# A gated delta rule in front of a mixture of experts: token-major rows with the head's parity on the partition halves

## The reference, cut to what matters

```python
q, k, v = (short_conv_silu(x @ W, conv) for W, conv in ...)   # x: layer-normed, 4 taps over tokens
q, k = l2norm(q), l2norm(k)                                   # per head
beta = sigmoid(x @ Wb)                                        # one number per token and head
for each token:                                               # the delta rule, state S is 64x64 per head
    u = beta * (v - k @ S);  S = S + outer(k, u);  o = (q / 8) @ S
o = o * rsqrt(mean(o * o) + 1e-5) * norm_w                    # per head
x = x + o @ Wo
x = x + experts(layernorm(x))                                 # 16 routed experts, top 4, and a shared one
```

## Time and profile before

| what | us |
|---|---|
| three runs | 1413.03, 1421.60, 1421.83; median 1421.6 |
| the profiled execution | 1421.09 |
| its span, first to last instruction | 1419.3 |
| around the span | 1.8 |
| TensorE busy | 1325.8 (93% of the span) |
| DVE busy | 865.7 (61%) |
| ACT busy | 372.2 (26%) |
| first hop, last hop (start of the first product) | 128.5, 604.4 |
| mean granted clock of TensorE | 0.963 of 2.4 GHz |

### The profile page before, as it was taken

The page is one execution under the profiler, slowest core; times in us unless marked ns, Lnnn a source line. Parts: engine busy times, 40 slices in busy tenths (PEclk is TensorE's granted clock), DMA queues, the critical chain, the costliest instruction groups (busy, mean ns, idle before and its releaser), DMA issues.

```text
span 1419.3 us, 27137 instructions
## 1 busy us (share of the span) xinstructions
PE 1325.8 (93%) x8434; PEld 836.9 (59%) x8435; DVE 865.7 (61%) x2394; ACT 372.2 (26%) x794; POOL 349.6 (25%) x422
## 2 busy tenths in 40 slices
PE   5968998999999779998999989999999999999996
PEld 4757776887687546554444445555555555555553
DVE  3797578458754711543511157777777777777774
ACT  3544545354454223312000001111111111111111
POOL 1202313132322212311455202122221222222211
PEclk9988999899898889999999999999999999999998
DMA  4204543754366961126545735666667555565430
GB/s 150 46 15 115 88 111 86 150 104 89 98 131 159 250 140 41 43 85 210 184 179 217 240 70 127 131 130 134 133 154 165 127 126 124 121 145 75 73 53 4
DMA packets 208386, 171.06 MB, mean 121 GB/s; under 512 B 71344, under 2 KB 160432, under 8 KB 208304
## 3 DMA queue, kind: packets, MB, share of 16 engines
q1 hardware_dynamic: 134928, 114.16, 30.1%
q0 software_dynamic: 16496, 34.23, 12.2%
q10 hardware_dynamic: 56880, 21.54, 7.3%
HBM read 91.06 MB, written 82.73 MB: 122 GB/s over the span
## 4 chain that ended last, share of the span: by engine, by line
PE 52%; DVE 1%; issue 1%; POOL 0%; POOLq 0%; ACT 0%; DVEq 0%
PE pD L2007 14%; PE pG L1989 13%; PE pU L1998 13%; PE pD L1977 4%; PE pG L1960 4%; PE pU L1960 3%; DVE ups L1907 1%; PE pU L1954 0%; PE pD L1974 0%; POOLq L1730 0%; DVE xsT L1895 0%; POOL front_region L1784 0%; DVE a L1930 0%; ACT y L1860 0%; ACT ups L1821 0%
## 5 line engine op out<-in xcount | busy, mean ns | idle before, releaser
L1907 DVE STREAM_TRANSPOSE ups<-a 32x96 f32<-32x96 f32 (+1 forms) x1264 | 330.3, 261 | 42.7
L1804 POOL DMA_INDIRECT out<-y,ix x79 | 122.6, 1551 | 491.7 <-ACT y L1860 338.2
L2007 PE MATMUL pD<-w,ups 128*128 (+1 forms) x474 | 219.3, 599 | 3.6 <-DVE ups L1907 3.6
L1989 PE MATMUL pG<-w,xsT 128*128 x632 | 201.5, 461 | 3.0 <-issue 3.0
L1998 PE MATMUL pU<-w,xsT 128*128 x632 | 199.9, 459 | 0.0
L1989 PEld LDWEIGHTS pG<-w,xsT 128*128 128x128 f32 x632 | 120.3, 190 | 92.5 <-issue 42.2
L882 PE MATMUL pProj<-front_region 128*128 128x256 f32 x624 | 162.8, 406 | 2.1 <-ACT front_region L665 1.5
L1998 PEld LDWEIGHTS pU<-w,xsT 128*128 128x128 f32 x632 | 120.1, 190 | 66.9
L2007 PEld LDWEIGHTS pD<-w,ups 128*128 128x128 f32 (+1 forms) x474 | 90.8, 192 | 98.0 <-issue 81.7
L1221 DVE SCALAR_TENSOR_TENSOR front_region<-front_region,cw 128x256 f32<-128x256 f32 x288 | 135.6, 512 | 14.9 <-ACT front_region L679 11.4
L882 PEld LDWEIGHTS pProj<-front_region 128*128 128x128 f32 x624 | 117.9, 198 | 21.9 <-ACT front_region L665 2.1
(11 more groups left out here) (238 smaller groups left out, 1610.5 us busy)
## 6 DMA issues: line engine op xcount, KB each, us to landing
w<-in_up_T SPq DMA_DIRECT2D x16, 1408.0 KB
slot_rows<-zeros SPq DMA_DIRECT2D x79, 266.0 KB
xs<-slot_rows ACTq DMA_DIRECT2D x316, 64.0 KB
w<-in_down_T SPq DMA_DIRECT2D x16, 512.0 KB
front_region<-in_L_attn_hidden_states SPq DMA_DIRECT2D x16, 256.0 KB, 3.6
x2r<-in_L_attn_hidden_states SPq DMA_DIRECT2D x16, 256.0 KB, 4.8
partial_sums<-x2r SPq DMA_DIRECT2D x16, 256.0 KB, 3.2
x_normed<-x2n SPq DMA_DIRECT2D x16, 256.0 KB, 2.2
```

The source lines that it names most:

```text
L1804: pool.indirect_dma_start(out=flat, out_offset=bass.IndirectOffsetOnAxis(ap=ix[1 - par][:, 0:1], axis=0), in_=y[1 - par][:, :], in_offset= ...
L1907: dve.transpose(aT[par][B * to:B * to + B, 0:n, rows], a[rows, 0:len(IC) * P].rearrange("p (c n) -> p c n", c=len(IC))[:, 0:n, B * to:B * ...
L1989: mm = pe.matmul(pG[0][:, 0:I], xsT[par][:, k, :], w[:, bass.ds(slot, 1), 2 * I * k:2 * I * k + I], start=(k == 0), stop=(k == DC - 1))
L2007: mm = pe.matmul(pYq[:, :], aT[1 - par][0:m, c, :], down[0:m, :, UPW + D * c:UPW + D * (c + 1)], start=(c == 0), stop=(c == 2))
```

## The change

Token-major rows get another layout: the partition is now (head's parity f, token within the chunk), and the chunk c lies on the free axis beside n. Everything that holds token-major rows follows: Rs, Us, osb, vh, ktok, NP, TT, PT, and PSUM pC and pG, where the bank is now picked by the chunk c and no longer by f.

- All hops' products read half f and write half f: the two quadrants on the diagonal, f = 0 and 1 in turn, both into bank c. `gram` and `scores` use these two quadrants as well.
- `residual`, `u_copy` and `o_copy` of a chunk are 128x256 and contiguous instead of 64x512 in two banks.
- Each turn of k, q, v and o is 16 products of 64x64 with the identity (an ordinary matmul, two records each, x32) instead of 4 transposes of 128x128 (x4).
- `betas` is 32 products for a pair, each with 64 tokens as the stationary operand and 4 columns moving, where it was 8 with 128 tokens and 8 columns. Wb's columns are permuted on the host.
- The semaphore QS_psum and the wait on it in `hop_o` go; the order of the three groups there stays.

```diff
+    def of_chunk(ap, c):
+        return ap[:, HH * DH * c:HH * DH * (c + 1)]
...
             def u_copy(t, c):
                 act.wait_ge(s_Up, 2 * t + c + 1)
                 least(act, s_Op, 2 * t + c - 1)
-                r = cols(c, C)
-                act.activation(Us[r, :].rearrange("p (f m) -> p f m", f=2), pC[r, :, 0:HH * DH], ACT.Copy).then_inc(s_U, 1)
+                act.activation(of_chunk(Us, c), pC[:, c, 0:HH * DH], ACT.Copy).then_inc(s_U, 1)
...
+            def turn_heads(bank_, src, done):
+                for n in range(HH):
+                    for c in range(2):
+                        for f in range(2):
+                            mm = pe.matmul(bank_[half(f), 0, cols(HH * c + n)], src(n, c, f), ident[half(f), half(f)],
+                                           start=True, stop=True)
+                mm.then_inc(done, 1)
...
                 for h in range(2):
-                    for k in range(DC):
-                        mm = pe.matmul(pT0[:, 0, H * h:H * h + H], xnT[p % 2][:, k, cols(h, P)], wb[:, k, :],
-                                       start=(k == 0), stop=(k == DC - 1))
+                    for c in range(2):
+                        at = H * h + HH * c
+                        for k in range(DC):
+                            for f in range(2):
+                                mm = pe.matmul(pT0[half(f), 0, at:at + HH], xnT[p % 2][:, k, tok(h, c)],
+                                               wb[:, k, HH * f:HH * f + HH], start=(k == 0), stop=(k == DC - 1))
...
-                turn(pT0, lambda m: kq[p % KQ_RING][:, m, tok(t)], s_ktp)
+                turn_heads(pT0, lambda n, c, f: kq[p % KQ_RING][half(f), n, tok(t, c)], s_ktp)
...
                     for c in range(2):
                         for f in range(2):
                             kk = kq[p % KQ_RING][half(f), n, tok(t, c)]
-                            mm = pe.matmul(pG[cols(c, C), f, cols(n)], kk, kk, start=True, stop=True)
+                            mm = pe.matmul(pG[half(f), c, cols(n)], kk, kk, start=True, stop=True)
...
             def hop_u(t, c):
                 pe.wait_ge(s_TT, t + 1)
                 pe.wait_ge(s_R, 2 * t + c + 1)
-                r = cols(c, C)
                 for n in range(HH):
+                    g = HH * c + n
                     for f in range(2):
-                        g = HH * f + n
-                        mm = pe.matmul(pC[r, f, cols(n)], TT[t % TT_RING][r, cols(g)], Rs[r, cols(g)], start=True, stop=True)
+                        mm = pe.matmul(pC[half(f), c, cols(n)], TT[t % TT_RING][half(f), cols(g)], Rs[half(f), cols(g)],
+                                       start=True, stop=True)
...
-                dve.tensor_tensor(half_major(Rs[r, :]), two_banks(pC, r), by_half(vh[t % VH_RING][r, :]), ALU.subtract)\
+                dve.tensor_tensor(of_chunk(Rs, c), pC[:, c, 0:HH * DH], of_chunk(vh[t % VH_RING], c), ALU.subtract)\
```

More of the change, by code:

```diff
@@ L341, in by_head, with by_chunk, two_banks @@
         return ap.rearrange("p (h d) -> p h d", d=DH)
[L343 to L351, removed]
+    def of_chunk(ap, c):
+        return ap[:, HH * DH * c:HH * DH * (c + 1)]
+    def by_chunk(ap):
+        return ap.rearrange("p (c n d) -> p c n d", c=2, d=DH)
+    def two_banks(ps):
+        return ps[:, :, 0:HH * DH].rearrange("p c (n d) -> p c n d", d=DH)
     def heads_of(ap, t, w=DH):
         one = ap[:, H * (t % 2):H * (t % 2) + H]
-        return one.rearrange("p (n f) -> p f n", f=2).unsqueeze(3).to_broadcast([P, 2, HH, w])
+        return one.rearrange("p (c n) -> p c n", c=2).unsqueeze(3).to_broadcast([P, 2, HH, w])
     def quads(ap):
@@ L736, in o_copy @@
                 least(act, s_oTp, t - 1)
-                r = cols(c, C)
-                act.activation(by_half(osb[t % 2][r, :]), two_banks(pC, r), ACT.Copy).then_inc(s_O, 1)
+                act.activation(of_chunk(osb[t % 2], c), pC[:, c, 0:HH * DH], ACT.Copy).then_inc(s_O, 1)
             def o_square(t):
@@ L908, in qT @@
                     pe.wait_ge(s_qsq, t)
-                turn(pT0, lambda m: kq[p % KQ_RING][:, DC + m, tok(t)], s_qtp)
+                turn_heads(pT0, lambda n, c, f: kq[p % KQ_RING][half(f), DC + n, tok(t, c)], s_qtp)
             def vT_turn(t):
@@ L918, in vT_turn @@
                     pe.wait_ge(s_vh, t)
-                turn(pT0, lambda m: vT[:, m, tok(t)], s_vtp)
+                turn_heads(pT0, lambda n, c, f: vT[half(f), n, tok(t, c)], s_vtp)
             def gram(t, u):
@@ L986, in hop_o @@
                 pe.wait_ge(s_U, 2 * t + c + 1)
-                r = cols(c, C)
                 for n in range(HH):
                     for f in range(2):
-                        mm = pe.matmul(pC[r, f, cols(n)], kq[t // 2 % KQ_RING][half(f), DC + n, tok(t, c)],
-                                       S[half(f), cols(n)], start=(n == 0), stop=False, skip_group_check=True)
-                mm.then_inc(s_QS, 1)
+                        pe.matmul(pC[half(f), c, cols(n)], kq[t // 2 % KQ_RING][half(f), DC + n, tok(t, c)],
+                                  S[half(f), cols(n)], start=(n == 0), stop=False, skip_group_check=True)
                 for n in range(HH):
+                    g = HH * c + n
                     for f in range(2):
-                        mm = pe.matmul(pS[half(f), 0, cols(n)], ktok[t % KT_RING][r, cols(2 * n + f)],
-                                       Us[r, cols(HH * f + n)], start=False, stop=False, skip_group_check=True)
+                        mm = pe.matmul(pS[half(f), 0, cols(n)], ktok[t % KT_RING][half(f), cols(g)], Us[half(f), cols(g)],
+                                       start=False, stop=False, skip_group_check=True)
                 mm.then_inc(s_Sp, 1)
-                for f in (c, 1 - c):
-                    if f != c:
-                        pe.wait_ge(s_QS, 2 * t + c + 1)
-                    for n in range(HH):
-                        g = HH * f + n
-                        mm = pe.matmul(pC[r, f, cols(n)], PT[t % 2][r, cols(g)], Us[r, cols(g)], start=False, stop=True,
-                                       skip_group_check=True)
+                for n in range(HH):
+                    g = HH * c + n
+                    for f in range(2):
+                        mm = pe.matmul(pC[half(f), c, cols(n)], PT[t % 2][half(f), cols(g)], Us[half(f), cols(g)],
+                                       start=False, stop=True, skip_group_check=True)
                 mm.then_inc(s_Op, 1)
@@ L1009, in oT_turn @@
                 least(pe, s_x2g, t)
-                turn(pT1, lambda c: osb[t % 2][:, cols(c, P)], s_oTp)
+                for n in range(HH):
+                    for c in range(2):
+                        for f in range(2):
+                            mm = pe.matmul(pT1[half(f), 0, P * n + C * c:P * n + C * c + C],
+                                           osb[t % 2][half(f), cols(HH * c + n)], ident[half(f), half(f)],
+                                           start=True, stop=True)
+                mm.then_inc(s_oTp, 1)
             def out_proj(t):
```

18 lines of the change are left out of this document (9 added, 9 removed).

## The result

| | before | after |
|---|---|---|
| median of 4 runs | 1417.3 | 1437.5 |
| lowest to highest | 1413.0 to 1421.8 | 1431.1 to 1440.7 |
| the profiled execution, its span | 1421.1, 1419.3 | 1431.1, 1429.3 |
| mean granted clock of TensorE | 0.963 | 0.973 |

The ratio is 1.0123, with a 95% interval of 1.009 to 1.0157. By the medians the change costs 15 to 20 us, 0.9 to 1.2%. The forecast was 1430, +8.7: the time lies in its range, on its upper side. The two profiled executions are 10.0 us apart, near the sum; the medians are about twice as far apart as it said.

A forecast was written before the change was run, and what follows sets the result against it. TensorE was taken to set the end in the hops' stretches, DVE during the first inverse. Terms +3 + 15.3 - 6 - 3.6 = +8.7 on the profiled 1421.1 gave 1430 us (own range 1420 to 1440, chance 0.52); overall range 1409 to 1450.

The forecast's parts named there:

- less than twice: Sign that the prediction is wrong: turns on TensorE costing less than twice what they did; 0.93 for 0.44 us was forecast.
- Betas didn't double: Rival: a pair's betas double to 3.7 us and no wait absorbs anything, 1447 us; chance 0.23.
- The halves of one bank don't block each other: Rival it answers: TensorE takes both row halves' products in one bank one after another, 1570 us; chance 0.05.
- the bounds set for them: Signs of being wrong: mean clock from 128 to 630 us moving over 0.02, last inverses' load wait changing over 5 us.
- I take half of those waits, -6: From 110.8 to 440 us, longer TensorE work and shorter Rs fill half of 11.2 us of waits; bounds 0 and -11.
- The third rival: Hops' chain and clock give back more than products cost: shorter waits, a third of clock loss regained, 1414 us; chance 0.20.
- +3 up to 60 us: Opening: four turns of k and two grams, plus shapes, stand ahead of DVE's scaling of the Gram matrices, +3 us.
- nothing from there to 110.8: From 60 to 110.8 us, 7 turns and two grams, some 5 us, lie beside DVE's dense work: nothing.
- the 15.3: Sum from 110.8 to 440 us: turns +20.6, scores and grams +10.1, hops -18.4, shapes +3, before waits.
- From 440 to 505 us nothing was forecast: Turns, grams, scores and hops there sum to +0.6, ahead of a 10.7 us wait set by DVE and transfers: nothing.
- The tail was to give 3.6: From 505 to 630 us: 8 hops -7.4, 5 turns +2.4, 3 scores +1.4, together -3.6 us.
- the 1400 us for the far end of the third: Third rival's far end: half the clock loss regained, tail hops gain 6 us more, 1400; chance beyond 1% faster 0.12.

The follow-up runs named there:

- e8: The changed kernel run again unchanged, 7 runs, as a baseline: 1435.7 us, ratio 1.0092 to before.
- e3: The changed kernel with the old wide betas (128 tokens stationary, 8 columns): 1427.1 us, ratio 1.0057 to before.
- e10: The kernel before with betas alone in the narrow form (64 tokens stationary, 4 columns): 1420.6 us, ratio 0.9982 to before.
- e7: The kernel before with PT Us of a tile's two chunks issued together in turn, one copy osb per tile: 1411.9 us, ratio 0.9935 to before.
- e9: The kernel before with each hop's PT Us issued in turn with the next hop's U: 1426.4 us, ratio 1.0017 to before.
- e11: e9 with the turn of o and its copy oT one slot later: 1418.3 us, ratio 0.9978 to before.
- e12: The kernel e7 run again beside e11: 1409.4 us, ratio 0.9907 to before.
- e6: The changed kernel with each copy Us and osb and each subtraction Rs doubled into an unread scratch tile: 1437.5 us, ratio 1.0105 to before.
- e2: The changed kernel with the turns of k, q and v doing only their first chunk: 1417.2 us, ratio 0.9975 to before.
- e4: The kernel before with each turn of k, q, v and o issued twice: 1439.4 us, ratio 1.0143 to before.
- e5: The changed kernel with every product of gram and scores issued twice: 1456.7 us, ratio 1.0237 to before.
- e1: The changed kernel with products of U and PT Us issued for all even heads, then all odd ones: 1444.5 us, ratio 1.0174 to before.

## Why the prediction came out as it did

**Right, by the rows above.** A quadrant's record costs 0.058 us, and the price of a group is its fullest quadrant: U and PT Us fell by 0.45 to 0.5, gram and scores rose by 0.4 to 0.5, a turn by 0.46 to 0.59, and q S with k Us stayed. A turn costs 2.3 times its old price against the 0.44 us between wide neighbours, but 1.9 times with a hop's R behind it (0.99 us, 343.56 to 344.55, for 0.53), so the sign "less than twice" depends on the neighbour; the added time is the forecast's. Betas didn't double (1.97 us with x64, not 3.7). Rs and the copies came out at the sizes given. The halves of one bank don't block each other: all the new groups write one bank from both halves. "TensorEngine Tiling (Array Packing)" of the Trainium skill (Restrictions and Gotchas, Gotcha 1), weighed in the prediction, has it otherwise; the measured 0.57 us of PT Us decides. The mean clock from 128 to 630 us went from 0.94 to 0.95 in both profiles, and the wait for the last inverses' load from 10.7 us to 9.5 (12.6 in e8): neither passed the bounds set for them.

**The step that failed: "I take half of those waits, -6".** The waits of the steady part did not shrink. Rs gave 3.4 us, as argued, but the load of the inverses took 4.5 back, and the sum rose by 1.0, 7 us from the -6. I had taken the wait for the load as something that longer work on TensorE fills. That would hold if DVE's inverse went on at its own pace; here DVE takes its pieces in the same list as the Rs of each hop, and may come later with them. That reason is argued and not shown; shown are the two waits.

**A second term, put at nothing, covered it: the clock.** The third rival said that longer turns and scores would keep TensorE's clock up, and that is what happened in the stretch of the hops, without the shorter waits that it joined to it: some 7 to 8.5 us of clock came back, where that rival had 11 and the forecast none. The marks of the profiles, with what the granted clock lacks to 1 added up from 125 to 640 us:

| profile | first hop | first to last hop | last hop to end | clock lacks |
|---|---|---|---|---|
| before | 128.5 | 475.9 | 814.9 | 32.4 |
| after | 140.1 | 477.3 | 811.9 | 25.6 |
| e8 | 137.3 | 479.1 | 814.7 | 23.9 |
| e3, wide betas | 136.1 | 471.2 | 814.7 | 18.8 |
| e10, before with narrow betas | 134.3 | 476.0 | 812.6 | 32.4 |

From the first hop to the last the forecast comes to 11.8 - 6 - 3.6 = +2.2 us, and +1.4 and +3.2 came. That is right by luck: waits that were to fall by 6 rose by 1 or 2, and the clock paid for it. Nor does it mean anything that the sum without the -6, +14.7 or 1435.8 us, lies where the medians of after do (1435.7 and 1437.5), since the profiles, from which the sum was made, are 10.0 and 11.8 apart. And the 3.0 us that the profile of after gains behind the last hop are within the scatter of that part, 810.5 to 818.4 us over the 14 profiles.

**The opening was a few us too small.** The forecast was +3 up to 60 us, nothing from there to 110.8, and some 3.5 of the 15.3 up to the first hop: about 6.5. It is 8.8 in e8 and 11.6 in after. The four other versions of before whose opening is untouched (e7, e9, e11, e12) reach their first hop at 128.4 to 130.0 us, so 1.5 us of such a distance can be the execution's. On DVE the marks are the scaling of tile 3's Gram matrix and the first vh behind the first inverse. Before:

```profile
64.37 0.68 DVE L1252 TENSOR_TENSOR NP<-pG,ng 128x512 f32<-128x512 f32 x1
...
110.11 0.68 DVE L1244 TENSOR_TENSOR vh<-pT,sqk 128x512 f32<-128x512 f32 x1
```

e8:

```profile
68.30 0.68 DVE L1265 TENSOR_TENSOR NP<-pG,ng 128x512 f32<-128x512 f32 x1
...
115.03 0.68 DVE L1257 TENSOR_TENSOR vh<-pT,sqk 128x512 f32<-128x512 f32 x1
```

+3.9 at the first and +4.9 at the second: the cover between 60 and 110 us held but for 1 us. The 3.9 more up to the first hop are the work counted into the 15.3, a bit dearer: the turn of v there takes 1.91 us for 0.91, both at the lower clock. What is left, 2.8 us in the profile of after, goes with the late rise of the clock; the forecast had nothing for it.

**The rest of the sum.** From the first hop to the 21st the shift grew by 5.1 and 7.1 us in the two profiles, where 11.8 of products remained after the opening's share and the waits gave 1 to 2 on top; the clock, whose mean over fixed times (128.5 to 440 us) went from 0.96 to 0.98 and in e8 to 0.97, made up 3 to 6 of the difference, and 2 or 3 us stay unexplained. From 440 to 505 us nothing was forecast, and +1.8 came (16.7 to 18.5, 15.9 to 17.7). The tail was to give 3.6 and gave 5.5 and 5.7 up to the last hop. Among the rivals, the 1400 us for the far end of the third adds up to 1402 or 1403 by its own terms (1430 - 16.5 - 5 - 6), which changes no chance.

**Off the path.** That Rs, Us and osb were worth little by themselves is shown by e6. That turns, grams and scores count on TensorE is shown by e2, e4 and e5, but at 64 to 86% of their length and not in full; the hops' own products count less, 7 to 12 of 18 us in e1. Applied to the whole change, as an estimate, this gives 21 to 27 of the 31.4 us of turns, about 10 of the 14.8 of grams and scores, and 12 to 20 of the 29.7 that U and PT Us save: +10 to +26, around the 15 to 20 measured. So the new layout loses because it adds 46 us to save 30, and by e1 less of the saving arrives than of what is added.

## What to carry to other kernels

Before a layout is changed so that products fill more quadrants of the array, look for two groups that already lie on different quadrants and issue their products in turn: it took half as much off TensorE here as the new layout's hops, and needed none of its turns. Count the turns first: four 128x128 transposes cost 0.44 us, the same turn by quadrants 1.0, and two turns per hop undo what two quadrants save. And a saved product is only worth its time if what it delays isn't waited for: e9 took twice as much from TensorE as e7 and gained nothing, because the result of one group came half a step later.

## What was not expected of the hardware

- Sixteen records on one quadrant take 1.02 us, in strict turns with another quadrant 0.52 to 0.57 (0.61 with a wide group behind U), and eight of one parity behind eight of the other 0.85 to 0.89 (e1). As these three read, records run beside each other only near where the quadrant changes.
- When TensorE's clock comes up at the start varies between executions of one program: a projection of 3.58 us at 26.74 in one, 1.84 at 24.96 in the other. It came late in 4 profiles of 7 with betas of 64 narrow records and in none of 7 with 16 wide ones. The granted clock reads 1.00 there in all of them.
- With the old grams, of 0.52 us, the granted clock fell to 0.50 behind betas and scores near 320 us whether betas were wide (before) or narrow (e10); with the new ones, of 1.03 us, it stayed at 1.00 in both forms (e3, after). Which of the longer groups keeps it up is not shown.
- In e9 and e11 four U groups with two interleaved operand pairs waited 8.9 and 9.9 us for nothing that the profile shows. No run tells what it is.
